# Last layer of a four-layer convolution network: GpSimd's strip copy behind the gate products, and the residual additions of the second unit ahead of the last product

## The reference

```python
def _L3_conv_ref(x, w_in, w_dw, fft_mask, w_out):
    y = jnp.einsum('oc,bchw->bohw', w_in, x)                    # 48 -> 288 channels
    yp = y.reshape(B, C2, ht, P, wt, P).transpose(0, 1, 2, 4, 3, 5)   # P = 8
    f = jnp.fft.rfft2(yp) * fft_mask[None]
    yp = jnp.fft.irfft2(f, s=(P, P))
    ...
    y = lax.conv_general_dilated(y, w_dw, ..., padding=((1, 1), (1, 1)), feature_group_count=C2)
    x1, x2 = jnp.split(y, 2, axis=1)                            # 144 channels each
    g = jax.nn.gelu(x1, approximate=False) * x2
    return jnp.einsum('oc,bchw->bohw', w_out, g)

# --- layer 3 (conv_preact) ---
x = x + _L3_conv_ref(_gn(x), L3_conv_w_in, L3_conv_w_dw, L3_conv_fft_mask, L3_conv_w_out)
```

## Time and profile before

| what | us |
|---|---|
| median of 3 runs | 13,136.62 (13,131.61 to 13,141.66) |
| the profiled execution, its own time | 13,145.65 |
| its span, first to last instruction | 13,143.1 |
| mean granted TensorE clock | 0.981 of full |

### The profile page before, as it was taken

One profiled execution on the slowest core, in us unless ns is written; L12 is line 12 of the kernel. 1 busy time (PEld: TensorE's weight loads), 2 busy tenths in 40 slices (PEclk: granted clock), 3 DMA queues, 4 the chain that ended last, 5 costly groups with the idle time before them and its releaser, 6 DMA issues. The chain is left out here.

```text
span 13143.1 us, 324877 instructions
## 1 busy us (share of the span) xinstructions
PE 12512.8 (95%) x130266; PEld 8457.9 (64%) x130266; DVE 8333.2 (63%) x17483; ACT 5538.0 (42%) x11157; POOL 4693.4 (36%) x3557
## 2 busy tenths in 40 slices
PE   7999899899989998999999999999998999999998
PEld 6877444577767775555555555555557887787777
DVE  0000677433335444888888888888876777777777
ACT  0000111211123333555455545555546676676666
POOL 0000222000000154566566666666653443333333
PEclk9999999999999998999999999999999999999999
DMA  4333566883755597565565555555642222222222
GB/s 128 133 133 128 134 158 160 160 152 72 155 126 154 159 228 166 77 80 79 79 80 81 79 79 80 80 79 80 79 65 71 51 51 54 53 52 49 54 50 48
DMA packets 2284445, 1306.11 MB, mean 99 GB/s; under 512 B 1877860, under 2 KB 2176219, under 8 KB 2197359
## 3 DMA queue, kind: packets, MB, share of 16 engines
q1 hardware_dynamic: 2015884, 1183.10, 45.4%
q10 hardware_dynamic: 267232, 104.65, 3.3%
HBM read 646.90 MB, written 450.74 MB: 84 GB/s over the span
## 5 line engine op out<-in xcount | busy, mean ns | idle before, releaser
L1578 PE MATMUL l_m<-l_wa,l_pix 128*128 128x288 f32 x8192 | 2210.8, 413 | 62.3 <-DMA l_left<-k_within_dram 59.1
L1440 POOL TENSOR_TENSOR l_qkv<-l_qkv,l_copies 128x576 f32<-128x576 f32 x1024 | 1438.9, 1405 | 1853.3 <-DVE l_qkv L1778 1853.3
L1578 PEld LDWEIGHTS l_m<-l_wa,l_pix 128*128 128x128 f32 x8192 | 1474.7, 190 | 757.7 <-issue 304.2
L1287 PE MATMUL l1h_ps<-l1h_ring,l1h_w 96*96 96x256 f32 x6120 | 1327.1, 379 | 50.0 <-ACT l1h_ring L1235 46.3
L1058 PE MATMUL l1v_ps<-l1v_rows,l1v_w 96*96 96x256 f32 x6120 | 1326.0, 378 | 31.9 <-ACT l1v_rows L1031 31.9
L1430 POOL TENSOR_TENSOR l_pix<-l_raw 128x516 f32<-128x516 f32 x1024 | 1258.2, 1229 | 25.1 <-DMA l_raw<-l_raw 25.1
L2096 PEld LDWEIGHTS l_e<-k_ident,l_turn 128*112 128x112 f32 x9900 | 1090.1, 135 | 257.7 <-issue 130.4
L2096 PE MATMUL l_e<-k_ident,l_turn 128*112 128x128 f32 x9900 | 1168.0, 277 | 92.3 <-DVE l_out L2258 85.6
L1287 PEld LDWEIGHTS l1h_ps<-l1h_ring,l1h_w 96*96 96x96 f32 x6120 | 998.9, 163 | 378.1 <-issue 46.7
L1058 PEld LDWEIGHTS l1v_ps<-l1v_rows,l1v_w 96*96 96x96 f32 x6120 | 990.5, 162 | 367.1 <-issue 31.0
L1271 POOL TENSOR_TENSOR l1h_columns<-l1h_blocks,l1h_ring 96x2048 f32<-96x2048 f32 x64 | 356.7, 5597 | 2417.9 <-DVE l1h_ring L1320 2417.9
(11 more groups left out here) (245 smaller groups left out, 22639.6 us busy)
## 6 DMA issues: line engine op xcount, KB each, us to landing
l0a_x<-x_px_dram SPq DMA_DIRECT2D x128, 1176.0 KB, 5.0
l0b_x<-x_in_dram SPq DMA_DIRECT2D x128, 493.8 KB
l_raw<-l_raw SPq DMA_DIRECT2D x128, 483.6 KB, 7.3
l_raw<-x_dram SPq DMA_DIRECT2D x1280, 48.0 KB, 3.7
l_x<-x3p_dram SPq DMA_DIRECT2D x132, 384.0 KB
l_out<-x_dram SPq DMA_DIRECT2D x528, 96.0 KB
out_dram<-l_out SPq DMA_DIRECT2D x132, 384.0 KB
x_dram<-l0b_out ACTq DMA_DIRECT2D x256, 193.5 KB, 3.1
```

Source lines behind the costliest of these rows:

```text
L1287: last = nc.tensor.matmul(ps[g][0:C2, 0:GI * V], w[:, kernel, s, :], ring[:, g, before % DEEP, :, s:s + V], start=(s == 0), stop=(s == 2))
L1440: nc.gpsimd.tensor_tensor(q, q, copies[:, g % 2, 1:2, :].broadcast_to([128, 2, OUTC]), ALU.add)\
L1578: return nc.tensor.matmul(bank[i][:, 0:OUTC], pix[:, k, i, first:first + 128], wa[:, b, i, :], start=True, stop=False)
```

## The change

Two things. GpSimd's strip copy of a unit gets one more wait: it begins when all four gate products of its unit are done. And in the program of unit 1 VectorE makes the two residual additions ahead of the fourth gate product and no longer behind it (in units 0 and 2 the order stays).

```diff
@@ def slab (vector) @@
                     if not (first and j == 0) and (j < 2 or last):
-                        for piece in (2, 3):
-                            gated(n if j else n - 1, j - 1 if j else 2, piece)
+                        gated(n if j else n - 1, j - 1 if j else 2, 2)
+                        if j != 1:
+                            gated(n if j else n - 1, j - 1 if j else 2, 3)
                     if j < 2 and not first:
                         for s in range(2):
                             residual(n, j, s)
+                    if j == 1:
+                        gated(n, 0, 3)
@@ def slab (gpsimd) @@
                     join(slice(2, PAIRS))
                     pool.wait_ge(joined, u * 4 + 4)
                     pool.wait_ge(added, u + 1)
+                    pool.wait_ge(gate_out, u * 4 + 4)
                     pool.sem_inc(saving, 1)
                     nc.gpsimd.tensor_copy(strip[:, j], inner(4)).then_inc(saved, 1)
```

## The result

| | before | changed |
|---|---|---|
| median of 4 runs, us | 13,139.1 (13,131.6 to 13,142.3) | 12,993.4 (12,985.1 to 12,994.6) |
| profiled execution, its own time, us | 13,145.65 | 12,992.26 |
| span, us | 13,143.1 | 12,989.9 |
| mean granted TensorE clock | 0.981 | 0.984 |

The ratio to before is 0.9889, 95% interval 0.9871 to 0.9906: 146 us, 1.1%, faster. Between the profiled executions it is 153.4 us, all of it in the last layer.

What follows compares the result with a forecast made beforehand. It took the last layer to be bound by TensorE's work plus about 206 us of waiting for VectorE. Terms 53 + 44 + 20 + 36 = 153 us gave 12,993 for the profiled execution, 12,984 as median; range 12,955 to 13,045.

Steps and rivals of the forecast that it cites:

- The stall: VectorE's gate products, held up by GpSimd's strip copy: 160 us of VectorE over 198 units, all of it should go.
- First unit: Wait before the projection in a slab's first unit: shorter by the whole stall, 65 x 0.81 = 53 us, bounds 0 and 56.
- Second unit: Transposes' wait for residual additions in a slab's second unit: down to a floor of 0.37 us, gain 44 us, bounds 0 and 56.
- The new order is worth nothing on top: Residual additions ahead of the last gate product in second units: no gain beside the copy's wait, and no cost.
- Third unit: Next slab's channel mix: its fourth matmul group starts 0.3 us earlier, 65 x 0.3 = 20 us, bounds 0 and 53.
- The clock: TensorE's lower clock in 22 first-unit projections costs 40 us; a shorter wait before them takes back 36, bounds 0 and 40.
- GpSimd's side: The later strip copy delays neither GpSimd's next joins nor VectorE's reads of PSUM: cost 0.
- The order alone: Rival: the copy doesn't matter to the slow product, only the new order acts, 39 us in second units, 13,098; chance 0.03.
- A contention that moves to the reads of PSUM: Rival: the copy holds up VectorE's PSUM reads by up to 1.04 us in second and third units; 13,066, chance 0.04.
- the rival on hidden waits: Rival: TensorE's own pauses, partly hidden now in waits for VectorE, eat gains; 13,052 at worst, 13,010 at half; chance 0.14.

Runs made afterwards that it cites:

- the kernel with `j == 2`: Kernel before, with the copy's new wait for the gate products put on the copies of third units alone: 13,065.6 us, ratio 0.9944.
- a third edit: Changed kernel, with TensorE's third group of transposes waiting for the first residual addition only, the fourth for both: 12,959.1 us, ratio 0.9854.

## Why the prediction was right, point by point

- *The total.* Predicted 12,984, measured 12,993.4. For the profiled execution the sum gave 12,993 and it took 12,992.3. That closeness is luck: the four terms were off by -6, -2, +5 and +4 us, and these cancel. The 9 us are the step from the one figure to the other: the profiled execution before was 9 us above the median, the one after is 1 below it. The prediction took this for a fixed offset; it was scatter.
- *The stall,* 160 us of VectorE: 154 went. The mechanism is shown: the two instructions block each other, as the traces of before had it and the copy behind the first product shows.
- *First unit,* 53 us: 46.6. The chain was right: the wait ahead of the projection, 2.02 us where the stall was whole and the convolution had no pause, is now 1.16, less by all of the 0.86. The price was not: it was the mean stall of all 198 units. Taking the stall out of first units alone brought the mean of 726 products from 898 to 830 ns (the kernel with `j == 2`), and that is 49 us. In 5 of the 65 units the turn read between the two products now waits for TensorE, 1.2 us in all.
- *Second unit,* 44 us: 42.2, with the floor of 0.37 us as read. *The new order is worth nothing on top:* 0.9891 without it and 0.9889 with it. That it costs nothing, with 0.1 us to spare, was right as well; once the 0.37 are gone it costs about 20 us.
- *Third unit,* 20 us: 24.6, half of it by luck. The step from the mix's third group to its fourth, on which the term rests, was 0.41 us in the one unit read, but 0.20 on the mean of 64: in all it went from 13.1 to 2.7 us, a gain of 10. The rest came from the mix's seventh and eighth groups (115.6 to 100.1 us together), where the prediction held TensorE to set the pace.
- *The clock,* 36 us: 40. The reason, the wait ahead of the projection, is shown from both sides. The estimate of where it sets in, above 1.41 us and by 1.66, read the wait without the pauses of the convolution ahead of it. With them every fall in the kernel before came after 2.00 us or more, and the shortest in any kernel after 1.64.
- *GpSimd's side,* 0: right, with 0.63 us to spare where 0.7 had been estimated.
- *The rivals.* The order alone was put at 13,098 and is 13,102, in part by chance: second units gave 33 us and not 39, and 14 came from fewer slow projections. A contention that moves to the reads of PSUM is refuted: in the changed kernel 133 spread reads lie beside the copy and take 689 ns on the mean, and in the kernel with the wait alone 148 residual additions do and take 687. This agrees with the Trainium skill, by which an instruction of VectorE with at most one SBUF input, outside the two-port modes, does not contend with GpSimd (SBUF — State Buffer, "Who interferes with whom").
- *Slips without effect.* Of the 22 slow projections two take 3.73 and 3.78 us, below the 3.8 given. Half of the way to 13,052, in the rival on hidden waits, is 13,018 and not 13,010.

## What to carry to other kernels

An instruction whose mean is above that of its twins of the same shape can hide a wait that no view of waits lists. Look in the timelines for the engine that runs beside it, and put that engine's work where this one has no such instruction. Price an edit together with the others: the new order was worth 40 us alone, nothing beside the wait, and about minus 20 beside a third edit. A wait for two things is worth splitting when the first waiter needs only the first. And a price taken from one unit, or from a mean over all kinds of units, should be checked against the mean of the very units it is for.

## What the runs showed of the hardware that was not expected

TensorE's granted clock fell to its lower level after waits of 1.35 to 2.02 us for a gate product. Counted with the pauses of the convolution just ahead, TensorE had then stood for at least 1.64 us, and at about 2.0 us some three first units in ten fell. The number of slow projections in the 65 first units follows the usual length of that stand: 22 before, 20 with the stall left in first units alone and 14 with the order alone (2.02 us), 13 with the copy behind the first product (1.81), 6 with the second product made later (1.64), none where it is 1.16 or less. The 22 cost 40 us, a quarter of what the change gained.

A VectorE product of two SBUF inputs and a GpSimd copy from SBUF block each other, and whichever starts later is the long one: the product 1.54 us in place of 0.68, or, which was not expected, the copy 1.54 in place of 1.04. The profile shows it in that instruction's own duration and as no idle time.
